# Attention on one core: value products in seven groups a stage instead of ten, with the slots of the exponentials reassigned

## The chip, the cores and the metric

The kernel runs on 1 core of one Trainium2 chip. The metric is the device time of one launch in microseconds (us), the median of several runs. Five engines work side by side and meet at semaphores: TensorE (PE in the rows; PEld is its weight load), VectorE (DVE), ScalarE (ACT), GpSimd (POOL) and SyncE (SP), whose queue issues all transfers.

## The reference, cut to what matters

One block of a transformer: modulated layer norm, latent attention over 1024 positions with 32 heads, a gated residual, a second modulated norm and a feed-forward block. The change touches the attention alone:

```python
scores = jnp.einsum('bqhd,bkhd->bhqk', q_full, k_full) * softmax_scale
scores = jnp.where(causal[None, None], scores, jnp.finfo(scores.dtype).min)
attn = jax.nn.softmax(scores, axis=-1)
out = jnp.einsum('bhqk,bkhd->bqhd', attn, v).reshape(B, S, H * VD)
return out @ wo.T
```

The values of a head are taken in the latent space of 32 numbers a key, so that a key tile's values are 128 keys by 32.

## The kernel before, in words

**Stages, steps, units.** The attention runs in 8 stages (w = 0 to 7), one for each group of 4 heads. A stage has 12 steps (`STEPS`), each one tile of 128 keys against one block of 512 queries. Steps 0 to 3 belong to the first query block, steps 4 to 11 to the second. Causality makes some narrow: their widths in queries are 512, 384, 256, 128 for steps 0 to 3, 512 for steps 4 to 8, and 384, 256, 128 for steps 9, 10, 11. A step is cut into units of 128 queries (times 4 heads, 512 columns), 36 a stage; unit n of a stage is `UNITS[n]`. Step 4 has units 10 to 13, step 5 has 14 to 17, step 6 has 18 to 21, step 7 has 22 to 25, step 8 has 26 to 29, step 9 has 30 to 32, step 10 has 33 and 34, step 11 has 35.

**One step's work.** TensorE makes the scores of a unit with three matmuls (lines 799, 802, 806). ScalarE turns one or two units at a time into exponentials (line 1117). TensorE multiplies them with the values (`values`, line 817): four heads in four bands of 32 rows of PSUM bank 4, each f32 matmul recorded as two instructions, so 8 for a step. VectorE adds the step's exponentials to a running sum (`add`, line 1461). The exponentials of steps 0 and 4 are written straight into the tile of the running sum (`SUM`), so the first addition, that of step 1 or step 5, changes a tile that `values` of step 0 or 4 must have read: it waits for them (`if kt == 1: dve.wait_ge(S_.pv, ...)`). All other steps share two slots (`PR[:, 0]` and `PR[:, 1]`), in turn; the exponential of a step waits until the step before it in its slot has been both multiplied (`S_.pv`) and added (`S_.ad`).

**The order.** Each engine follows one list. In unit n, TensorE does the scores of the unit, then the value products that fall due (`VALUES[n]`, three units after the end of their step, and a step of width 256 held back to go with the next), then side work from a table (`TABLES[w][n]`); VectorE does the additions due (`SUMS[n]`, two units after the end of the step), then the same side work. Before the change `VALUES` stands in ten places of a stage: at unit 2 steps 10 and 11 of the stage before, at 6 step 0, at 9 step 1, at 12 steps 2 and 3, at 16 step 4, at 20 step 5, at 24 step 6, at 28 step 7, at 32 step 8, at 35 step 9.

**Side work.** In stages 0 to 6 it finds the row maxima of the next stage: 38 parts (line 736), each reduced from PSUM by VectorE (line 1369); eight of them are diagonal, and go over ScalarE (line 1062), a mask on GpSimd (line 1703) and VectorE ("least", line 1374). "even", "odd", "lat" and "split" make and rotate the queries of the stage after next, with products on GpSimd ("rotate", lines 1674 and 1675; `split_low`, line 1710). "den" sums the exponentials over the keys (line 749), VectorE copies and inverts the sums (lines 1393, 1398, 1400; "inv"), GpSimd multiplies the result with them ("norm", line 1716). Results of side work on TensorE take three PSUM banks in turn; a piece waits until the piece three places before has been read. "join" and "rows" close the maxima and send them on. A planner (`window_table`) lays the pieces out by a wished place and an estimated cost for VectorE, and moves each "den" to the next unit that has value products.

**Queries rotate in one buffer.** "even" on VectorE waits for `split_low` of the half before (`S_.tl`), since both use `RT`.

Of the kernel before, what the change touches and what calls it, by code (L numbers as in the profile page):

```python
# [14 lines left out]
P = 128  # L15
# [4 lines left out]
G, HG = 8, 4  # L20
# [12 lines left out]
STEPS = [(qb, kt) for qb in range(NQB) for kt in range((qb + 1) * QB // P)]  # L33
NSTEP = len(STEPS)
ADDS = [s for s in range(NSTEP) if STEPS[s][1] > 0]
NADD = len(ADDS)
# [67 lines left out]
def width(s):  # L104
    qb, kt = STEPS[s]
    return min(QB, (qb + 1) * QB - kt * P)


def units_of(s):
    return width(s) // P  # L110
# [13 lines left out]
UNITS = [(s, i) for s in range(NSTEP) for i in range(units_of(s))]  # L124
NUNIT = len(UNITS)
VALUE_LAG, ADD_LAG = 3, 2

HELD = [s for s in range(NSTEP - 1) if units_of(s) == 2]  # L130


def due(n, lag, held=()):

    after = [s + 1 if s in held else s for s in range(NSTEP)]
    return [((n - lag) // NUNIT * -1, s) for s in range(NSTEP)
            if UNITS.index((after[s], units_of(after[s]) - 1)) == (n - lag) % NUNIT]


VALUES = [due(n, VALUE_LAG, HELD) for n in range(NUNIT)]  # L140
SUMS = [due(n, ADD_LAG) for n in range(NUNIT)]
LATE_VALUES = [s for n in range(NUNIT) for ago, s in VALUES[n] if ago]
LATE_SUMS = [s for n in range(NUNIT) for ago, s in SUMS[n] if ago]


def blocks_of(qb):
    return (qb + 1) * QB // P
# [57 lines left out]
class Memory:  # L205
# [167 lines left out]

    def slot(self, s):
        qb, kt = STEPS[s]
        return self.SUM[qb] if kt == 0 else self.PR[:, ADDS.index(s) % 2]

    def out_of(self, g, qb):
        return self.attn[:, g, qb * QB:(qb + 1) * QB]
# [28 lines left out]
def group_places(g, places):  # L408

    return [(place, (name[0], g) + name[1:], 0.0 if name[0] in ("even", "odd") and g in HANDED else busy)  # L410
            for place, name, busy in places]


def window_table(w):

    places = []
    if w == G - 1:
        places += group_places(w, [(0.06 + 0.1 * m, ("fold", m), 1.3) for m in range(G)])
        places += group_places(w, [(0.3 + 0.3 * n, ("gate", n), 2.5) for n in range(2)])
        places += group_places(w, [(0.84 + 0.06 * st, ("high", st), 0.0) for st in range(2)])  # L420
        places += group_places(w, [(0.40 + 0.10 * d, ("mod", 2, d), 0.6) for d in range(KD)])
    else:
        places += group_places(w + 1, maxima_places(0.03, 0.76))
        if w < G - 2:
            places += group_places(w + 2, QUERY_PLACES)
    if w > 0:
        places += [(0.15, ("den", w - 1, 1), 0.7), (0.16, ("inv", w - 1, 1), 0.8), (0.24, ("norm", w - 1, 1), 0.0)]
    places += [(0.42, ("den", w, 0), 0.7), (0.43, ("inv", w, 0), 0.8), (0.50, ("norm", w, 0), 0.0)]
    places.sort(key=lambda x: x[0])
    table = []  # L430
    free = 0.0
    for n in range(NUNIT):
        place = (n + 1) / NUNIT
        for ago, s in SUMS[n]:
            if s in ADDS:
                free = max(free, place) + (HG * width(s) / 960 + 0.07) / WINDOW_US
        names = []
        while places and (n == NUNIT - 1 or max(places[0][0], free - SLACK) <= place):
            _, name, busy = places.pop(0)
            names.append(name)  # L440
            free = max(free, place) + busy / WINDOW_US
        table.append(names)

    for n in range(NUNIT):
        for name in [x for x in table[n] if x[0] == "den"]:
            inverse = ("inv",) + name[1:]
            for names in table:
                if inverse in names:
                    names.remove(inverse)
            table[n].remove(name)  # L450
            m = min(m for m in range(n, NUNIT) if VALUES[m])
            table[m] = [name] + table[m] + [inverse]
    return table


TABLES = [window_table(w) for w in range(G)]
FIRST_FOLDS = [("w", 0)]
FIRST_QUERIES = [[(kind, 0, hf) for kind in ("even", "odd", "lat", "split")] for hf in range(2)]
# [187 lines left out]
def pe_program(nc, M, PS, S_):  # L646
# [163 lines left out]
    def values(w, s):  # L810
        qb, kt = STEPS[s]
        wd = width(s)
        pe.wait_ge(S_.p, NEXP * w + LAST_EXP[s] + 1)
        if kt == 0 and 2 * w + qb > 0:
            pe.wait_ge(S_.o, 2 * w + qb)
        for h in range(HG):
            ins = pe.matmul(PS[h * L:(h + 1) * L, 4, QB - wd:QB], M.V[:, kt, :], M.slot(s)[:, h, 0:wd],  # L817
                            start=(kt == 0), stop=(kt == blocks_of(qb) - 1))
        ins.then_inc(S_.pv, 1)
# [31 lines left out]
    for w in range(G):  # L851
        for n, (s, i) in enumerate(UNITS):
            scores(w, s, i)
            for ago, before in VALUES[n]:
                if ago <= w:
                    values(w - ago, before)
            for name in TABLES[w][n]:
                side(name)

# [26 lines left out]
    for b in range(3):  # L886
        pe.wait_ge(S_.free[b], (len(TURN) + 1 - b) // 3)
    for n, s in enumerate(LATE_VALUES):
        product_term(0, n)
        values(G - 1, s)  # L890
    product_term(1, 0)
    for n in range(len(LATE_VALUES), 3):
        product_term(0, n)
# [66 lines left out]
def act_program(nc, t, M, PS, S_):  # L960
    act = nc.scalar
# [139 lines left out]
    def exponentials(w, e):  # L1101
        s, i, n = EXPS[e]
        qb, kt = STEPS[s]
        turn = NEXP * w + e
        act.wait_ge(S_.sc, turn + 1)
        if i == 0 and kt == 0:
            if w > 0:
                act.wait_ge(S_.side, (DEN0, DEN1)[qb][w - 1] + 1)
        elif i == 0:
            j = ADDS.index(s)  # L1110
            before = NSTEP * w + ADDS[j - 2] - (NSTEP if j < 2 else 0)
            if before > 0:
                act.wait_ge(S_.pv, before + 1)
                act.wait_ge(S_.ad, NADD * w + j - 1)
        banks = PS[:, 2 * (turn % 2):2 * (turn % 2) + n, :].rearrange("p u (h q) -> p u h q", q=P)
        tiles = M.slot(s)[:, :, i * P:(i + n) * P].rearrange("p h (u q) -> p u h q", q=P)
        act.activation(tiles, banks, ACT.Exp).then_inc(S_.p, 1)  # L1117
# [28 lines left out]
    for w in range(G):  # L1146
        for n, (s, i) in enumerate(UNITS):
            e = FIRST_EXP[s] + i // 2
            if i + 1 == EXPS[e][1] + EXPS[e][2]:
                exponentials(w, e)  # L1150
            for ago, before in VALUES[n]:
                if ago <= w and before in (3, NSTEP - 1):
                    empty(w - ago, STEPS[before][0])
            for name in TABLES[w][n]:
                side(name)
# [88 lines left out]
def dve_program(nc, M, PS, S_):  # L1244
# [259 lines left out]
    for w in range(G):  # L1504
        for n in range(NUNIT):
            for ago, s in SUMS[n]:
                if ago <= w and s in ADDS:
# [345 lines left out]
```

## Time and profile before

| | us |
|---|---|
| median of 3 runs (765.14 to 765.54) | 765.2 |
| the profiled execution, its own time | 766.67 |
| its span, first to last instruction | 764.5 |
| TensorE busy in the span | 731.0 (96%) |
| VectorE busy | 542.0 (71%) |
| ScalarE busy | 326.7 (43%) |
| GpSimd busy | 215.4 (28%) |

The busy shares are averages over the whole launch. The granted clock of TensorE is 0.997 of full speed over the span. The eight stages lie between about 90 and 534 us; what follows them is the output projection and the feed-forward block, which the change doesn't touch. In a timeline row the first number is the start, the second the length from first start to last end of the merged instructions, the number behind x their count, and a bracket tells for how long the engine had been idle and which instruction released it. Records of one engine overlap a little, so the time that an instruction takes up is best read from one start to the next.

### The profile page before, as it was taken

The page shows a single profiled execution, that of the slowest core. Times are in us where ns is not written, and L with a number is a line of the kernel's source. Part 1 is how long each engine was busy: PE and PEld are TensorE (multiplying, and loading weights), DVE is VectorE, ACT ScalarE, POOL GpSimd, SP SyncE. Part 2 cuts the span into 40 slices and gives each one's busy share as a digit, 9 for nine tenths or more (in the row PEclk, how much of TensorE's full clock was granted, in tenths as well). Part 3 has the DMA queues.
Part 4 walks back from the last instruction along what each step waited for, and adds up shares of the span by engine and source line. Part 5 has one row for each costly group of instructions (what it writes and reads, how often), then busy time and mean ns, then how long its engine had stood idle before and what let it go on. Part 6 is the DMA issues. An engine that isn't in the chain of part 4 may idle for free.

```text
span 764.5 us, 10504 instructions
## 1 busy us (share of the span) xinstructions
PE 731.0 (96%) x3867; PEld 509.8 (67%) x3867; DVE 542.0 (71%) x803; ACT 326.7 (43%) x499; POOL 215.4 (28%) x196
## 2 busy tenths in 40 slices
PE   3989999999999999999999999999999999999998
PEld 2856676666666666666666666555788888887886
DVE  6867678888888888888888889688695333223432
ACT  4744455545545545545545544444254322222210
POOL 1137635235235235225226121010264000000211
PEclk9999999999999999999999999999999999999999
DMA  8934553303303403303403390360200421200011
GB/s 312 250 72 94 120 118 84 89 11 84 88 12 83 93 7 84 90 11 84 97 3 83 84 358 1 111 220 1 82 23 7 123 71 54 76 10 1 29 41 42
DMA packets 39057, 63.15 MB, mean 83 GB/s; under 512 B 4384, under 2 KB 19232, under 8 KB 37152
## 3 DMA queue, kind: packets, MB, share of 16 engines
q1 hardware_dynamic: 39008, 62.49, 30.3%
q8 instruction: 32, 0.52, 0.3%
q14 instruction: 17, 0.14, 0.1%
HBM read 32.72 MB, written 2.10 MB: 46 GB/s over the span
## 4 chain that ended last, share of the span: by engine, by line
PE 69%; DVE 25%; issue 3%; ACT 2%; DMA 1%; POOL 0%; SPq 0%; DVEq 0%; ACTq 0%; POOLq 0%
PE PS L907 16%; PE PS L924 8%; PE PS L736 8%; DVE PR L1461 7%; PE PS L799 6%; PE PS L817 6%; PE PS L806 5%; PE PS L802 5%; PE PS L871 5%; DVE NMa L1369 4%; DVE wide L1461 3%; PE PS L727 3%; DVE NMd L1374 2%; PE PS L749 2%; PE PS L780 1%
## 5 line engine op out<-in xcount | busy, mean ns | idle before, releaser
L1117 ACT ACTIVATE PR<-PS 128x1024 f32<-128x1024 f32 (+1 forms) x144 | 133.2, 930 | 147.7 <-PE PS L806 116.3
L736 PE MATMUL PS<-KH,Q 96*128 96x128 f32 (+3 forms) x576 | 130.5, 327 | 10.9 <-DVE NMa L1369 5.3
L1369 DVE TENSOR_REDUCE NMa<-PS 128x1 f32<-128x512 f32 (+3 forms) x184 | 116.5, 656 | 29.3 <-PE PS L736 27.4
L736 PEld LDWEIGHTS PS<-KH,Q 96*128 96x128 f32 x576 | 88.8, 190 | 67.3 <-issue 30.7
L799 PE MATMUL PS<-Q,KH 96*128 96x512 f32 x288 | 119.2, 414 | 0.0
L1461 DVE TENSOR_TENSOR PR<-PR 128x2048 f32<-128x2048 f32 (+3 forms) x56 | 112.0, 2000 | 3.9 <-ACT PR L1117 1.5
L806 PE MATMUL PS<-Q,KH 97*128 97x512 f32 (+1 forms) x288 | 114.5, 398 | 0.0
L802 PE MATMUL PS<-Q,KL 96*128 96x512 f32 (+1 forms) x288 | 114.2, 396 | 0.0
L1703 POOL TENSOR_SCALAR_AFFINE_SELECT diag<-diag 128x512 f32<-128x512 f32 x64 | 47.6, 743 | 198.0 <-ACT diag L1062 197.9
L799 PEld LDWEIGHTS PS<-Q,KH 96*128 96x128 f32 x288 | 54.8, 190 | 27.7 <-issue 14.3
L817 PE MATMUL PS<-PR,V 128*32 128x512 f32 (+3 forms) x704 | 70.2, 486 | 0.0
L1585 DVE SCALAR_TENSOR_TENSOR wide<-PS,ffn_s,TQ 128x1024 f32<-128x1024 f32 x10 | 12.8, 1283 | 72.2 <-PE PS L907 72.2
L806 PEld LDWEIGHTS PS<-Q,KH 97*128 97x128 f32 (+1 forms) x288 | 54.6, 190 | 13.2 <-DMA Q<-NM 0.4
L802 PEld LDWEIGHTS PS<-Q,KL 96*128 96x128 f32 (+1 forms) x288 | 54.7, 190 | 8.3
L1062 ACT ACTIVATE diag<-PS 128x512 f32<-128x512 f32 x64 | 38.0, 594 | 46.3 <-PE PS L736 46.3
L907 PE MATMUL PS<-Q 128*128 128x512 f32 x240 | 55.5, 389 | 0.0
L1716 POOL TENSOR_TENSOR wide<-wide,RD 128x512 f32<-128x512 f32 x16 | 34.6, 2164 | 67.4 <-DVE RD L1400 67.4
L1777 POOL TENSOR_TENSOR OT<-TQ,Y 128x512 f32<-128x512 f32 x7 | 9.1, 1294 | 156.7 <-DVE Y L1606 156.7
L907 PEld LDWEIGHTS PS<-Q 128*128 128x128 f32 x240 | 45.0, 188 | 9.3
L907 PE MATMUL PS<-Q,KH 128*128 128x512 f32 (+1 forms) x192 | 49.1, 391 | 0.0
L1374 DVE TENSOR_REDUCE NMd<-diag 128x4 f32<-128x512 f32 x64 | 43.1, 674 | 0.0
L924 PE MATMUL PS<-DH,Q 128*128 128x512 f32 (+1 forms) x176 | 42.6, 390 | 0.0
(185 smaller groups left out, 1088.3 us busy)
## 6 DMA issues: line engine op xcount, KB each, us to landing
Q<-TQ SPq DMA_DIRECT2D x64, 384.0 KB, 6.2
RT<-in_wo SPq DMA_DIRECT2D x4, 1024.0 KB, 4.9
TQ<-in_wo SPq DMA_DIRECT2D x4, 1024.0 KB, 4.8
WI<-in_gate_w SPq DMA_DIRECT2D x10, 256.0 KB, 3.4
WI<-in_up_w SPq DMA_DIRECT2D x10, 256.0 KB, 3.8
DI<-in_down_w SPq DMA_DIRECT2D x10, 256.0 KB, 2.8
PR<-in_wmod_c SPq DMA_DIRECT2D x2, 1024.0 KB, 6.3
x_in<-in_x SPq DMA_DIRECT2D x8, 256.0 KB, 9.7
```

Source lines behind the costliest of these rows:

```text
L736: ins = pe.matmul(bank[:, i * w:(i + 1) * w], M.Q[0:KR, g % 2, 0, qt // 4, h0 + i, qs], M.KH[0:KR, lo:lo + w], start=(i == 0), stop=(i == ...
L799: pe.matmul(dst, M.KH[0:KR, ks], M.Q[0:KR, w % 2, 0, qb, :, qs], start=True, stop=False)
L802: pe.matmul(dst, M.KL[0:rows, ks], M.Q[0:rows, w % 2, 0, qb, :, qs], start=False, stop=False)
L806: ins = pe.matmul(dst, M.KH[0:rows, ks], M.Q[0:rows, w % 2, 1, qb, :, qs], start=False, stop=True)
L817: ins = pe.matmul(PS[h * L:(h + 1) * L, 4, QB - wd:QB], M.V[:, kt, :], M.slot(s)[:, h, 0:wd], start=(kt == 0), stop=(kt == blocks_of(qb) - 1))
L907: ins = pe.matmul(PS[0:m, 4 * b + 2 * w + hf, :], a[b][:, w, k, 0:m], h[:, k, hf * 512:(hf + 1) * 512], start=(n == 0 and k == 0), stop=(n ...
L924: ins = pe.matmul(PS[:, 4 + b, :], a[b][0:k, ch, :], w[0:k, ch, :], start=(n == 0 and ch == 0), stop=(n == 2 and rest == 1))
L1117: act.activation(tiles, banks, ACT.Exp).then_inc(S_.p, 1)
L1369: dve.tensor_reduce(dst, PS[:, bank_of(turn), 0:n * w].rearrange("p (h k) -> p h k", k=w), axis=AX.X, op=ALU.max, negate=True).then_inc(S_ ...
L1374: dve.tensor_reduce(M.NMd[:, qt // 4, :, qt % 4], M.diag[:, qt % 2], axis=AX.X, op=ALU.max, negate=True).then_inc(S_.dm, 1)
L1461: dve.tensor_tensor(sums, sums, M.slot(s)[:, :, 0:wd], ALU.add).then_inc(S_.ad, 1)
L1703: pool.affine_select(out=tile, in_=tile, compare_op=ALU.is_ge, fill=MASKED, base=0, pattern=[[0, HG], [-1, P]], channel_multiplier=1).then ...
```

## The change

Value products stand in seven places of a stage: at unit 2 steps 9, 10 and 11 of the stage before, at 6 step 0, at 12 steps 1, 2 and 3, at 20 steps 4 and 5, at 24 step 6, at 28 step 7, at 32 step 8. In the last stage step 9 stays at unit 35 (`LAST_HELD`).

The two slots are used in another order: one by steps 1, 5, 7, 9, the other by steps 2 and 3 together (side by side, 256 and 128 queries), 6, 8, and 10 and 11 together. So the exponentials of steps 3 and 11 wait for nobody, that of 5 waits for step 1 in place of 2, and those of the others for the same step as before.

The addition of step 5 comes four units after the end of its step 4, at unit 21 in place of 19 (`add_lag`), since the values of step 4 are now taken at unit 20 in place of 16.

The planner's answer follows. In stages 0 to 5 "den" of the first block and its inversion go from unit 16 to unit 20; "least 4", part 24 and "odd" of the second half go from units 20 and 21 to unit 19; parts 25 and 26 from units 21 and 22 to unit 20; "norm" from unit 21 to unit 26, behind `split_low` on GpSimd. Stages 6 and 7 have the same move of "den" and small shifts around it.

```diff
-HELD = [s for s in range(NSTEP - 1) if units_of(s) == 2]
...
+WITH = {1: 3, 2: 3, 4: 5, 9: 11, 10: 11}
+LAST_HELD = 9
+
+SLOTS = ((1, 5, 7, 9), ((2, 3), 6, 8, (10, 11)))
+
+
+def slot_of(s):
+    return 0 if s in SLOTS[0] else 1
+
+
+def used_before(s):
+
+    uses = [use if isinstance(use, tuple) else (use,) for use in SLOTS[slot_of(s)]]
+    n = [s in use for use in uses].index(True)
+    return (uses[n - 1][-1], 1 if n == 0 else 0) if s == uses[n][0] else None
+
+
+def add_lag(s):
+
+    return VALUE_LAG + 1 if STEPS[s][1] == 1 and WITH.get(s - 1) == s else ADD_LAG
...
+VALUES = [due(n, lambda s: VALUE_LAG, WITH) for n in range(NUNIT)]
+SUMS = [due(n, add_lag) for n in range(NUNIT)]
+LATE_VALUES = [s for n in range(NUNIT) for ago, s in VALUES[n] if ago and s != LAST_HELD]
...
-        return self.SUM[qb] if kt == 0 else self.PR[:, ADDS.index(s) % 2]
+        if kt == 0:
+            return self.SUM[qb]
+        lo = 0 if units_of(s) > 1 else 2 * P
+        return self.PR[:, slot_of(s), :, lo:lo + width(s)]
...
-    places += [(0.42, ("den", w, 0), 0.7), (0.43, ("inv", w, 0), 0.8), (0.50, ("norm", w, 0), 0.0)]
+    places += [(0.42, ("den", w, 0), 0.7), (0.43, ("inv", w, 0), 0.8), (0.64, ("norm", w, 0), 0.0)]
...
+            if (w, n) == (G - 1, NUNIT - 1):
+                values(w, LAST_HELD)
...
-        elif i == 0:
-            j = ADDS.index(s)
-            before = NSTEP * w + ADDS[j - 2] - (NSTEP if j < 2 else 0)
-            if before > 0:
-                act.wait_ge(S_.pv, before + 1)
-                act.wait_ge(S_.ad, NADD * w + j - 1)
+        elif i == 0 and used_before(s):
+            before, ago = used_before(s)
+            if w >= ago:
+                act.wait_ge(S_.pv, NSTEP * (w - ago) + before + 1)
+                act.wait_ge(S_.ad, NADD * (w - ago) + ADDS.index(before) + 1)
```

## Rows read from the trace of the kernel before

**Rows 1.** The page: busy time by engine; the chain that ended last, by engine.
```profile
PE 731.0 (96%) x3867; PEld 509.8 (67%) x3867; DVE 542.0 (71%) x803; ACT 326.7 (43%) x499; POOL 215.4 (28%) x196
...
PE 69%; DVE 25%; issue 3%; ACT 2%; DMA 1%; POOL 0%; SPq 0%; DVEq 0%; ACTq 0%; POOLq 0%
```

**Rows 2.** Windows: stage 3, and VectorE's stretch in it; length, then busy PE, PEld, DVE, ACT, POOL.
```profile
259.13:316.27 57.14, 55.58 (x324) 36.29 (x320) 49.92 (x67) 28.77 (x38) 21.64 (x17) 1.00 0.26 60
288.40:312.80 24.40, 23.42 (x121) 15.34 (x121) 23.32 (x32) 12.12 (x15) 13.42 (x9) 1.00 0.29 65
```

**Rows 3.** Timeline of TensorE: value groups at units 12 and 20 of stage 3.
```profile
279.16 0.86 PE L817 MATMUL PS<-PR,V 128*32 128x256 f32 x16
279.95 0.73 PE L736 MATMUL PS<-KH,Q 96*128 96x512 f32 x2
...
292.79 0.39 PE L806 MATMUL PS<-Q,KH 97*128 97x512 f32 x1
293.11 1.06 PE L817 MATMUL PS<-PR,V 128*32 128x512 f32 x8
294.10 0.50 PE L799 MATMUL PS<-Q,KH 96*128 96x512 f32 x1
294.44 0.39 PE L802 MATMUL PS<-Q,KL 96*128 96x512 f32 x1
```

**Rows 4.** Timeline of TensorE: the wait in unit 13, and unit 16 of stage 3.
```profile
281.95 0.66 PE L736 MATMUL PS<-KH,Q 96*128 96x128 f32 x4 [0.57 <-DVE RT L1343]
...
285.88 0.40 PE L802 MATMUL PS<-Q,KL 96*128 96x512 f32 x1
286.11 0.39 PE L806 MATMUL PS<-Q,KH 97*128 97x512 f32 x1
286.43 1.07 PE L817 MATMUL PS<-PR,V 128*32 128x512 f32 x8
287.32 1.04 PE L749 MATMUL PS<-wide,ones 128*32 128x512 f32 x8
288.29 0.94 PE L736 MATMUL PS<-KH,Q 96*128 96x128 f32 x5
```

**Rows 5.** Timeline of VectorE: the first stretch without idle time of stage 3.
```profile
270.49 0.72 DVE L1393 STREAM_TRANSPOSE RD<-PS 128x512 f32<-128x512 f32 x1 [1.49 <-PE PS L749]
...
280.62 0.68 DVE L1342 TENSOR_TENSOR RT<-PS,sin 128x512 f32<-128x512 f32 x1
281.22 0.67 DVE L1343 TENSOR_TENSOR RT<-PS,cos 128x512 f32<-128x512 f32 x1
```

**Rows 6.** Timeline of VectorE: units 16 to 35 of stage 3.
```profile
288.43 0.72 DVE L1393 STREAM_TRANSPOSE RD<-PS 128x512 f32<-128x512 f32 x1 [1.08 <-PE PS L749]
...
293.40 2.28 DVE L1461 TENSOR_TENSOR PR<-PR 128x2048 f32<-128x2048 f32 x1
...
299.92 2.46 DVE L1461 TENSOR_TENSOR PR<-PR 128x2048 f32<-128x2048 f32 x1
...
305.88 3.41 DVE L1461 TENSOR_TENSOR PR<-PR 128x2048 f32<-128x2048 f32 x1
...
310.74 0.67 DVE L1374 TENSOR_REDUCE NMd<-diag 128x4 f32<-128x512 f32 x1
...
312.79 5.47 DVE L1461 TENSOR_TENSOR PR<-PR 128x2048 f32<-128x2048 f32 x3
```

**Rows 7.** Timeline of ScalarE: the exponential of step 10 in stage 3.
```profile
315.19 1.03 ACT L1117 ACTIVATE PR<-PS 128x1024 f32<-128x1024 f32 x1 [1.42 <-DVE PR L1461]
```

**Rows 8.** Timeline of GpSimd in stage 3.
```profile
287.51 2.42 POOL L1710 TENSOR_TENSOR TQ<-RT,TQ 128x1024 fp32r<-128x1024 f32 x1 [2.35 <-ACT TQ L1071]
...
298.94 1.29 POOL L1675 TENSOR_TENSOR RT<-RT 128x512 f32<-128x512 f32 x1
300.18 3.35 POOL L1716 TENSOR_TENSOR wide<-wide,RD 128x512 f32<-128x512 f32 x1
...
304.72 2.42 POOL L1710 TENSOR_TENSOR TQ<-RT,TQ 128x1024 fp32r<-128x1024 f32 x1 [0.31 <-ACT TQ L1071]
```

More of the change, by code:

```diff
@@ L126, with due @@
 VALUE_LAG, ADD_LAG = 3, 2
-HELD = [s for s in range(NSTEP - 1) if units_of(s) == 2]
[L133 to L142, printed above, removed]
+WITH = {1: 3, 2: 3, 4: 5, 9: 11, 10: 11}
[9 more added lines that the diff above has]
+    return VALUE_LAG + 1 if STEPS[s][1] == 1 and WITH.get(s - 1) == s else ADD_LAG
+def due(n, lag, held={}):
+    after = [held.get(s, s) for s in range(NSTEP)]
+    return [((n - lag(s)) // NUNIT * -1, s) for s in range(NSTEP)
+            if UNITS.index((after[s], units_of(after[s]) - 1)) == (n - lag(s)) % NUNIT]
+VALUES = [due(n, lambda s: VALUE_LAG, WITH) for n in range(NUNIT)]
+SUMS = [due(n, add_lag) for n in range(NUNIT)]
+LATE_VALUES = [s for n in range(NUNIT) for ago, s in VALUES[n] if ago and s != LAST_HELD]
 LATE_SUMS = [s for n in range(NUNIT) for ago, s in SUMS[n] if ago]
```

## The prediction, made before the changed kernel ran

> **What bounds the kernel now.** I read the page first [rows 1]: TensorE is busy 96% of the span, yet a quarter of the chain that ended last lies on VectorE. So TensorE is nearly always occupied, but some of its pace is set by VectorE. Then the windows [rows 2]: a stage takes 57.14 us, with VectorE busy for 49.92 of it. In the 24.40 us from unit 16 to the end of unit 32 it is busy for 23.32: there it has 1.08 us to spare, and TensorE has about as much (23.42 busy). Last I followed stage 3 row by row. Three links carry the stage round:
>
> - The first scores of a stage need the bank that the exponential of step 10 empties. That exponential starts when VectorE has added step 8, whose slot it takes, at 315.19, and ends at 316.22 [rows 7]. The next stage begins at 316.27 [rows 2]. TensorE's own work, with the values of step 9 as its last piece, ends at the same moment.
> - "den" of the stage before, at unit 6, starts a stretch of VectorE without a gap from 270.49 to 281.8 [rows 5], after which TensorE has waited 0.57 us for a bank in unit 13 [rows 4].
> - "den" of unit 16 is copied at 288.43, and 24.36 us later, at 312.79, VectorE starts the addition of step 8 [rows 6], which leads to the first link.
>
> **What a group costs.** Ordinary matmuls follow each other every 0.23 us [rows 4]. A 512-wide step followed at once by "den" takes 0.89 us (286.43 to 287.32), so 128 queries cost 0.22. Between ordinary matmuls, the step of unit 20 takes 1.65 from 292.79 to 294.44 [rows 3]; less two ordinary ones (0.46) and the step itself (0.88) this leaves 0.31 us for going into the narrow form and out again. The pair of unit 12 takes 0.79 for 384 queries [rows 3], no more than its columns and one passage need. A group of three is not in the trace; its joints cost between nothing and 0.31 each, and by the pair I take nothing. The bands of 32 are a tiling mode, and the Trainium skill (TensorEngine Tiling (Array Packing), Key Properties) says that changing the mode drains TensorE; the trace agrees with its 0.31.
>
> Fewer groups remove passages at units 9, 16 and 35 in stages 0 to 6. In stage 7 a "fold" in the same narrow form stands behind the values at 9 and 16, and step 9 stays at 35, so nothing is removed there. That is 21 passages, 6.5 us of TensorE, if nobody else sets the pace.
>
> **Where that goes: the start of a stage.** The values of step 9 (384 queries, 0.66 us) leave unit 35 and enter unit 2. At the boundary their leaving gives nothing, since the exponential of step 10 ends at 316.22 anyway. In unit 2 they lengthen a stretch that TensorE paces: VectorE had been idle 1.49 us when "den" reached it [rows 5]. So "den" comes 0.65 us later, VectorE's stretch ends 0.65 later, and unit 13 resumes at 282.60 in place of 281.95. The passage saved at unit 9 only lengthens the wait in unit 13.
>
> **The middle.** Unit 16 ends its scores at 286.34 + 0.65 = 286.99 (one pitch behind 286.11 [rows 4]) and has no values or "den". What stood between 288.29 and 293.11, the parts of units 16 to 18, "even" and the scores of units 17 to 20, takes 4.82 - 0.10 of passage. Part 24 and "odd" join in unit 19: four matmuls of 128 columns and three of 512, about 1.15 us (an estimate from 0.1 and 0.23 each and the joints). One wait is near: "even" may not start before the first half's `split_low` has ended. That was 289.93 [rows 8], becomes 290.58, and comes about 0.45 later than "even" would like; before it was no limit. So the values of step 4 start at about 286.99 + 4.72 + 1.15 + 0.10 + 0.45 = 293.4. From there to VectorE's copy of "den" it was 2.00 us (286.43 to 288.43); with step 5 in between it is 2.88. The copy starts at 296.3.
>
> VectorE meanwhile does "even" from 290.65, part 23, "least 4" and "odd": six instructions at 0.60 from start to start [rows 5], until 294.3. Here it used to add step 5 (293.40 [rows 6]). That addition must now wait for the values of step 4, which have moved from unit 16 to unit 20, and the queue puts it at unit 21, behind "den". VectorE stands still for 2.0 us, in the half of the stage where it had 1.08 to spare. This is the step on which the forecast turns.
>
> From the copy to the addition of step 8: 24.36 before. Parts 21, 22, 23, "even", "least 4" and "odd" now lie ahead of it (eight instructions at 0.60, and 0.05 between two: -4.9). The 1.08 idle goes, as the pieces are ready by then. The additions of steps 6 and 7 took 2.46 and 3.41 against 2.28 for that of step 5 [rows 6], because two-operand work of VectorE and GpSimd on SBUF excludes each other: that of step 6 began when rotation ended at 300.23, that of step 7 when `split_low` ended at 307.14 [rows 8]. Rotation is now earlier (-0.18), and `split_low` ends just as VectorE comes to step 7 (-1.13). "norm" follows `split_low` on GpSimd now, then the mask of the last diagonal, so "least 7" waits some 0.3. Sum: 24.36 - 4.9 - 1.08 - 1.31 + 0.3 = 17.4; the addition of step 8 starts at 313.7 in place of 312.8, and the stage is 0.85 us longer. TensorE keeps up; its saved passages turn into waiting. The sending of the maxima at the end of the stage is shifted with VectorE and stays covered.
>
> **The sum.** Stages 1 to 5: 5 x 0.85 = 4.25. Stage 0 has nothing at unit 2: 0.85 - 0.65 = 0.2. Stage 6 has no queries to rotate and a freer VectorE: between all of TensorE's gain (-0.93 for three passages, -0.66 for step 9 handed on) and +0.85; midway, -0.4. Stage 7 takes over step 9 (+0.65), and the late addition of step 5 holds up the exponential of step 7 for between 0 and 1.1 (what exclusion by "norm" costs, 3.41 less 2.28); I take 0.4. Together +5.1 us: span 764.5 to 769.6, the profiled time 766.67 to about 771.8. The profiled execution lies 1.5 above the median, so the median goes from 765.2 to 770.3.
>
> **The rivals.**
> - *TensorE's gain arrives* (faster). If VectorE can absorb its gap, all 21 passages count: 765.2 - 6.5 = 758.7. For it: TensorE is 96% busy, and exponentials 3 and 11 lose their waits. Against it: 23.32 of 24.40, and the boundary at 316.22. It decides if "den" of unit 20 is copied before about 294.5, so that the gap stays under 0.3 us. Then stages 1 to 5 end 0.9 us or more earlier than I have them.
> - *It cancels.* Half of the gap is made up: 1.0 less a stage for five stages gives 765.3.
> - *"norm" gets in first* (slower still). VectorE reaches step 7 at the very time when `split_low` ends. At 300.23 the waiting addition got ahead of a "norm" that stood behind rotation (its record starts at 300.18 and runs 3.35 [rows 8]). If the addition comes a moment too late, "norm" goes first: +1.29 for it, less the 0.3 of "least 7", in stages 0 to 5: 770.3 + 6 = 776.3. The Trainium skill (SBUF — State Buffer, SBUF: two separate sides) states that whichever starts first has the shared pair of ports for the whole instruction; the order at 300.23 agrees, since the addition had been issued first, and by it the outcome hangs on less than 0.3 us.
>
> **How the numbers follow.** Within 0.2% (763.7 to 766.7) is about what measurement can't tell from no change. My case has 0.40 and a range of its own of 767 to 773; "norm" first 0.16; TensorE's gain wholly or in part 0.28; cancelled 0.16. Below 760 I see 0.10 and above 776 another 0.09, so the range is 760 to 776. Faster 0.28, same 0.16, slower 0.56.
>
> **What the changed profile would show.** Right: in stages 1 to 5 a period near 58.0 in place of 57.14; VectorE idle about 2 us before L1393 of unit 20; the addition of step 5 about 5 us later in the stage; TensorE waiting some 0.8 us before the first scores of a stage; TensorE's busy time 5 to 6 us lower. "norm" first: the addition of step 7 at 3.4 us or more while L1716 runs. Wrong: no gap at unit 20, or a period of 56.5 or less. What would make it wrong above all: side work that VectorE finds ready in unit 19 and 20 later than I have it on TensorE's clock, or earlier.

## The result, and the profile after

The changed kernel takes 786.5 us (median of 4 runs, 784.18 to 786.74) where the kernel before took 765.2. The ratio is 1.0271, with a 95% interval of 1.0258 to 1.0284: slower by 21 us, and outside the range of 760 to 776. The profiled execution took 786.35 us with a span of 784.1, so the span grew by 19.6 us. The page after has these rows against those of [rows 1]: busy time by engine, and the last chain by engine.

```profile
PE 732.1 (93%) x3867; PEld 514.2 (66%) x3867; DVE 539.1 (69%) x803; ACT 323.9 (41%) x499; POOL 214.3 (27%) x196
...
PE 64%; DVE 25%; issue 4%; ACT 4%; POOL 2%; DMA 1%; SPq 0%; DVEq 0%; ACTq 0%; POOLq 0%
```

TensorE fell from 96% to 93% of the span: it waits more. Its busy time did not fall by the 5 to 6 us that fewer passages should have given; it rose by 1.1. The windows of stages 3 and 4 show why (length, busy PE, PEld, DVE, ACT, POOL, then the granted clock of TensorE):

```profile
266.70:325.70 59.00, 54.81 (x321) 36.73 (x320) 48.83 (x66) 28.34 (x38) 20.67 (x17) 1.00 0.26 60
325.70:386.00 60.30, 56.40 (x321) 37.25 (x320) 50.30 (x68) 28.34 (x38) 20.68 (x17) 0.97 0.26 59
```

In stage 3 TensorE is busy 54.81 us, 0.77 less than in [rows 2], where three passages at the forecast price would be 0.93. But the stage takes 59.0 where it took 57.14. Stage 4 is another 1.3 us longer and is the only one of the two with a mean clock below 1.00. These are two separate losses.

**The gap at unit 20 came as forecast.** VectorE in stage 3 after, to be held against [rows 6]:

```profile
297.62 0.69 DVE L1356 TENSOR_TENSOR RT<-PS,cos 128x512 f32<-128x512 f32 x1 [1.20 <-POOL TQ L1731]
...
300.61 0.68 DVE L1364 TENSOR_TENSOR RT<-PS,cos 128x512 f32<-128x512 f32 x1
303.42 0.72 DVE L1414 STREAM_TRANSPOSE RD<-PS 128x512 f32<-128x512 f32 x1 [2.12 <-PE PS L769]
...
306.13 2.25 DVE L1482 TENSOR_TENSOR PR<-PR 128x2048 f32<-128x2048 f32 x1
...
308.90 2.28 DVE L1482 TENSOR_TENSOR PR<-PR 128x2048 f32<-128x2048 f32 x1
...
314.68 3.42 DVE L1482 TENSOR_TENSOR PR<-PR 128x2048 f32<-128x2048 f32 x1
...
321.60 5.48 DVE L1482 TENSOR_TENSOR PR<-PR 128x2048 f32<-128x2048 f32 x3
```

Line 1482 is the addition (1461 before) and 1414 the copy of "den" (1393 before). VectorE is idle 2.12 us before the copy. (The 1.20 before "even", line 1356, is its wait for the `split_low` of the half before; the prediction had 0.45.) The additions of steps 5 and 6 take 2.25 and 2.28, unhindered. That of step 7 takes 3.42. GpSimd at that moment:

```profile
312.29 2.42 POOL L1731 TENSOR_TENSOR TQ<-RT,TQ 128x1024 fp32r<-128x1024 f32 x1
314.67 1.28 POOL L1737 TENSOR_TENSOR wide<-wide,RD 128x512 f32<-128x512 f32 x1
316.40 2.19 POOL L1724 TENSOR_SCALAR_AFFINE_SELECT diag<-diag 128x512 f32<-128x512 f32 x1 [0.45 <-ACT diag L1084]
```

The record of "norm" (line 1737) begins where `split_low` (line 1731) ends, at 314.67, and VectorE's addition begins at 314.68. "norm" takes its usual 1.28 us and the addition takes 1.14 more than the one before. All six stages with a `split` (0 to 5) show the same: the record of "norm" begins 0.01 to 0.03 us ahead of the addition's, and the addition takes 3.40 to 3.42. This is the rival *"norm" gets in first*, to which I had given 0.16 and a time of 776.3.

**The granted clock falls.** TensorE in stage 2, and the windows of 3.4 us on both sides of 260.2:

```profile
258.48 0.91 PE L756 MATMUL PS<-KH,Q 96*128 96x384 f32 x2 [1.17 <-DVE NMa L1390]
...
259.93 0.39 PE L819 MATMUL PS<-Q,KH 96*128 96x512 f32 x1
...
260.52 0.63 PE L826 MATMUL PS<-Q,KH 97*128 97x512 f32 x1
261.08 1.94 PE L837 MATMUL PS<-PR,V 128*32 128x512 f32 x8
```
```profile
256.80:260.20 3.40, 2.21 (x10) 1.33 (x9) 3.40 (x6) 0.60 (x2) 1.53 (x1) 1.00 0.00 0
260.20:263.60 3.40, 3.40 (x14) 0.99 (x13) 3.23 (x5) 1.77 (x3) 0.00 (x0) 0.50 0.02 5
```

TensorE waited 1.17 us for a reduction of VectorE, in unit 30. Soon after, the clock goes from full speed (2.4 GHz) to half (1.2 GHz) for 3.4 us: a matmul takes 0.63 instead of 0.39, the eight of step 8 take 1.94 instead of 1.06. It happens in stages 0, 2 and 4 (at 140.8, 260.2 and 379.7), and in stage 6 it lasts twice 3.4 us (from 461.6). The profiled execution of the kernel before had one such fall, in stage 6 at 465.9. Stages 1, 3 and 5 have a like wait (1.18, 1.18 and 1.15) and no fall. How many falls there are also differs between executions of one program: three of the four after have a mean clock of 0.988 or 0.989 and take 786.35 to 786.74 us, the fourth has 0.993 and takes 784.18.

### The profile page after: what moved, and what is told of

It reads as the page before. It is cut to its first block, busy times and chain, and to the rows that moved or that the text cites. A ratio compares the mean times of both kernels' runs of the same rounds, so it can differ in the third digit from the quotient of the medians.

```text
span 784.1 us, 10487 instructions
## 1 busy us (share of the span) xinstructions
PE 732.1 (93%) x3867; PEld 514.2 (66%) x3867; DVE 539.1 (69%) x803; ACT 323.9 (41%) x499; POOL 214.3 (27%) x196
## 4 chain that ended last, share of the span: by engine, by line
PE 64%; DVE 25%; issue 4%; ACT 4%; POOL 2%; DMA 1%; SPq 0%; DVEq 0%; ACTq 0%; POOLq 0%
PE PS L929 15%; DVE PR L1482 8%; PE PS L946 8%; PE PS L837 7%; PE PS L756 6%; PE PS L819 5%; PE PS L893 5%; DVE NMa L1390 4%; PE PS L826 4%; PE PS L822 4%; PE PS L747 3%; DVE wide L1482 2%; POOL TQ L1731 2%; PE PS L769 2%; DVE NMb L1390 2%
## 5 line engine op out<-in xcount | busy, mean ns | idle before, releaser
L756 PE MATMUL PS<-KH,Q 96*128 96x128 f32 (+3 forms) x576 | 128.0, 327 | 22.2 <-DVE NMa L1390 14.5
L1482 DVE TENSOR_TENSOR PR<-PR 128x2048 f32<-128x2048 f32 (+3 forms) x56 | 109.0, 1946 | 4.8 <-ACT PR L1138 2.7
L1724 POOL TENSOR_SCALAR_AFFINE_SELECT diag<-diag 128x512 f32<-128x512 f32 x64 | 54.9, 858 | 205.0 <-ACT diag L1084 205.0
L1737 POOL TENSOR_TENSOR wide<-wide,RD 128x512 f32<-128x512 f32 x16 | 25.7, 1606 | 69.2 <-DVE RD L1421 69.2
```

The costliest lines, as they stand in the source:

```text
L756: ins = pe.matmul(bank[:, i * w:(i + 1) * w], M.Q[0:KR, g % 2, 0, qt // 4, h0 + i, qs], M.KH[0:KR, lo:lo + w], start=(i == 0), stop=(i == ...
L1482: dve.tensor_tensor(sums, sums, M.slot(s)[:, :, 0:wd], ALU.add).then_inc(S_.ad, 1)
L1724: pool.affine_select(out=tile, in_=tile, compare_op=ALU.is_ge, fill=MASKED, base=0, pattern=[[0, HG], [-1, P]], channel_multiplier=1).then ...
```

## The experiments

I measured a stage by the time from one copy of the second block's "den" (unit 6) to the next. The first column is the start of the first of these copies; all in us.

| kernel | first | stage 1 | 2 | 3 | 4 | 5 | 6 | 7 | half clock in stages |
|---|---|---|---|---|---|---|---|---|---|
| before | 156.17 | 57.16 | 57.16 | 57.13 | 57.13 | 56.23 | 52.40 | 45.55 | 6 |
| after | 158.76 | 59.02 | 60.27 | 59.02 | 60.24 | 58.06 | 55.55 | 47.59 | 0, 2, 4, 6 (twice as long) |
| step 4 apart | 156.61 | 57.82 | 57.80 | 57.79 | 57.79 | 56.90 | 53.07 | 45.56 | 6 |
| "norm" late | 157.06 | 57.86 | 57.85 | 57.89 | 57.90 | 56.94 | 53.99 | 47.62 | 6 |
| waits filled | 157.87 | 58.96 | 58.97 | 58.97 | 58.96 | 58.06 | 54.94 | 47.62 | 6 |
| step 9 at home | 156.77 | 59.90 | 58.33 | 58.34 | 59.87 | 57.41 | 53.73 | 47.62 | 1, 4, 6 |
| `split` late | 154.93 | 56.03 | 56.04 | 56.01 | 56.02 | 55.12 | 50.86 | 45.58 | none |

The last column is what one profiled execution shows, not a constant of the kernel. A copy's period is named by the stage in which it begins, so the fall in stage 2, at 260.2, lies in the period of 60.27, and that of stage 0 in the first column.

**1. The joining of steps 4 and 5 undone** (`b_step4_apart`). The changed kernel without `4: 5`; "norm" goes back to its old place.

```diff
-WITH = {1: 3, 2: 3, 4: 5, 9: 11, 10: 11}
+WITH = {1: 3, 2: 3, 9: 11, 10: 11}
...
-    places += [(0.42, ("den", w, 0), 0.7), (0.43, ("inv", w, 0), 0.8), (0.64, ("norm", w, 0), 0.0)]
+    places += [(0.42, ("den", w, 0), 0.7), (0.43, ("inv", w, 0), 0.8), (0.50, ("norm", w, 0), 0.0)]
```

> The changed kernel, but the values of step 4 back at unit 16, the addition of step 5 back at unit 19, den at 16 and norm at 21 as before: eight groups a stage; steps 1 to 3 stay together at unit 12 and steps 9 to 11 at unit 2. Theory (VectorE's 2.1 us of standing still at unit 20, the exclusion by norm and the falls of TensorE's clock that follow TensorE's waits make the loss): VectorE has no gap at unit 20, and a stage costs only the 0.65 us of step 9 at unit 2: about 57.8 a stage in place of 57.14, no fall of the clock in stages 0 to 5, 767 to 770 us. Rival (the handing of step 9 over the stage's boundary is the main loss): 780 us or more.

Measured: 770.48 us, ratio 1.0063 (1.0048 to 1.0078). The stage takes 57.80 us, the gap before the copy is back at 1.09, and the falls of stages 0, 2 and 4 are gone. So three quarters of the loss come with the joining of steps 4 and 5 and with the place that "norm" then has, and what is left, 0.65 us a stage, is step 9 in unit 2, the term that I had for it. The collision of the kernel before is still in this kernel: its addition of step 7 takes 3.41.

**2. Step 9 at home** (`c_step9_home`). The opposite: steps 4 and 5 joined, step 9 at unit 35 in every stage, `LAST_HELD` gone.

```diff
-WITH = {1: 3, 2: 3, 4: 5, 9: 11, 10: 11}
+WITH = {1: 3, 2: 3, 4: 5, 10: 11}
```

> The changed kernel, but the values of step 9 back at unit 35 of their own stage: eight groups a stage; steps 4 and 5 stay together at unit 20. Theory: stages 1 to 5 get back 0.65 us each and stage 7 as much, VectorE's gap of 2.1 us at unit 20 stays: 781 to 784 us. Rival (step 9 over the boundary is the main loss): 765 to 770 us.

Measured: 780.11, ratio 1.0194 (1.0179 to 1.0209). A stage without a fall takes 58.33, 0.69 less than after. The time lies 0.9 under the range that I had expected; this profiled execution has two falls in stages 0 to 5, that of the changed kernel three. The falls are now in stages 1 and 4: they move with the timing, and aren't tied to certain stages.

**3. "norm" behind the last mask** (`d_norm_late`). All of the change, but "norm" of the first block moves from unit 26 to unit 28, behind part 32, in stages 0 to 5, and from unit 24 to 25 in stage 6.

```diff
-    places += [(0.42, ("den", w, 0), 0.7), (0.43, ("inv", w, 0), 0.8), (0.64, ("norm", w, 0), 0.0)]
+    places += [(0.42, ("den", w, 0), 0.7), (0.43, ("inv", w, 0), 0.8), (0.66, ("norm", w, 0), 0.0)]
```

> The changed kernel with norm of the first block one place later in stages 0 to 5, behind the mask of the last diagonal on GpSimd (unit 28 in place of 26), so that it can't stand between split_low and the addition of step 7. Theory: the addition of step 7 takes 2.3 us in place of 3.4, each of these stages is 1.0 us shorter (58.0 in place of 59.0): 780.5 us; if the shorter wait of TensorE behind it also does away with the falls of its clock, 776.5 us. Rival (norm's place doesn't matter, the loss lies in VectorE's gap alone): 786 us.

Measured: 775.40, ratio 1.0128 (1.0113 to 1.0143): 11.1 us faster than the change as it stood, with one number moved. That is 1.1 more than I had expected even without falls; stage 6, which I had left out, gained 0.95. VectorE and then GpSimd in stage 3 of this kernel:

```profile
307.02 1.88 DVE L1390 TENSOR_REDUCE NMa<-PS 128x1 f32<-128x512 f32 x3
308.81 0.68 DVE L1395 TENSOR_REDUCE NMd<-diag 128x4 f32<-128x512 f32 x1
309.40 2.28 DVE L1482 TENSOR_TENSOR PR<-PR 128x2048 f32<-128x2048 f32 x1
...
314.87 0.18 DVE L1402 TENSOR_TENSOR NMa<-NMa,NMb 128x16 f32<-128x16 f32 x1
```
```profile
307.02 2.41 POOL L1731 TENSOR_TENSOR TQ<-RT,TQ 128x1024 fp32r<-128x1024 f32 x1
311.12 1.06 POOL L1724 TENSOR_SCALAR_AFFINE_SELECT diag<-diag 128x512 f32<-128x512 f32 x1 [1.69 <-ACT diag L1084]
312.15 1.27 POOL L1737 TENSOR_TENSOR wide<-wide,RD 128x512 f32<-128x512 f32 x1
```

`split_low` ends at 309.43, and the addition of step 7 takes 2.28. From the copy of "den" to the addition of step 8 VectorE needs 17.05 us (298.14 to 315.19); I had summed 17.4. In the changed kernel it is 18.18 (303.42 to 321.60), longer by the 1.13 of exclusion. With that gone, TensorE's wait of 1.17 at unit 30 is gone too (no wait of 0.5 us or more is left there), and stages 0 to 5 of the profiled execution have no fall. Waits of 0.7 to 0.94 elsewhere in these stages stay. Two of the four executions have a clock of 0.994 and 0.995, lower than the 0.997 of the profiled one.

**4. TensorE's waits filled** (`e_fill`). The changed kernel, with matmuls into a free PSUM bank just before the waits: three at unit 26 and four at unit 30, in stages 0 to 6. Their results are overwritten by the scores that belong there; the computation is unchanged.

```diff
+            if n in (26, 30) and w < G - 1:
+                turn = NEXP * w + FIRST_EXP[s]
+                for _ in range(3 if n == 26 else 4):
+                    pe.matmul(PS[:, 2 * (turn % 2) + 1, :], M.KH[0:KR, 0:P], M.Q[0:KR, w % 2, 0, 1, :, 0:P], start=True, stop=True)
```

> The changed kernel with 3 matmuls more at unit 26 and 4 more at unit 30 in stages 0 to 6, into the bank that the next unit's scores overwrite; they lie in TensorE's waits for VectorE of 0.8 and 1.2 us there. Theory (the three falls of the clock to half speed in stages 0, 2 and 4 come of these waits and cost 1.25 us each): no fall in stages 0 to 5, the stages take 59.0 each without exception: 782 to 784 us. Rival (the falls have nothing to do with the waits): they stay, and the extra work costs nothing or a little: 786 to 789 us.

Measured: 782.15, ratio 1.0220 (1.0203 to 1.0237), 4.35 us faster than the change with more work on TensorE. TensorE in stage 3, with the four added matmuls in the first row:

```profile
315.14 1.09 PE L882 MATMUL PS<-Q,KH 96*128 96x512 f32 x4
316.45 0.91 PE L756 MATMUL PS<-KH,Q 96*128 96x384 f32 x2 [0.21 <-DVE NMa L1395]
```

All stages 1 to 4 now take 58.96 to 58.97. Against 60.27 and 60.24 that is 1.3 us a fall. VectorE's chain was not made shorter, so this price is the clock's alone. (In experiment 2 a fall costs 1.5 to 1.6: 59.90 and 59.87 against 58.33.) The fall of stage 6, behind a wait of 1.40 that was not filled, stays. The four executions have clocks of 0.996 to 0.998, against 0.988 to 0.993 of the change.

**5. `split` of the kernel before moved** (`h_split_late`). The exclusion at step 7 is already there in the kernel before: 3.41 us in [rows 6], where the addition came upon the `split_low` that starts at 304.72 [rows 8]. Here is the kernel before with one number changed, so that `split` of the second half stands behind part 32 in unit 28:

```diff
-                 (0.47, ("even", 1), 1.2), (0.50, ("odd", 1), 1.2), (0.55, ("lat", 1), 1.3), (0.60, ("split", 1), 0.0)]
+                 (0.47, ("even", 1), 1.2), (0.50, ("odd", 1), 1.2), (0.55, ("lat", 1), 1.3), (0.66, ("split", 1), 0.0)]
```

> The kernel before, its values untouched, but split of the second half on ScalarE and GpSimd behind the mask of the last diagonal (unit 28 in place of 26) in stages 0 to 5, so that it does not exclude the addition of step 7. Theory (VectorE sets the pace from unit 17 to 32): that addition takes 2.3 us in place of 3.4, and as TensorE has 0.75 and 0.21 us of waits there to give back, each of six stages is 0.7 to 1.0 us shorter: 759.5 to 761 us. Rival (TensorE sets the pace, exclusion of VectorE is hidden): 765 us.

Measured: 758.28, ratio 0.9906 (0.9892 to 0.9919). This kernel beats both, and lies 1.2 under my range. Its stage 3, VectorE and GpSimd:

```profile
302.40 2.27 DVE L1461 TENSOR_TENSOR PR<-PR 128x2048 f32<-128x2048 f32 x1
```
```profile
304.52 0.64 POOL L1703 TENSOR_SCALAR_AFFINE_SELECT diag<-diag 128x512 f32<-128x512 f32 x1 [3.58 <-ACT diag L1062]
305.47 2.42 POOL L1710 TENSOR_TENSOR TQ<-RT,TQ 128x1024 fp32r<-128x1024 f32 x1 [0.31 <-ACT TQ L1071]
```

The addition takes 1.14 less, and the stage 1.1 less (56.03). So these 1.1 us of VectorE's are 1.1 us of the stage, with no change in the work of TensorE.

**6. One passage more, where TensorE sets the pace** (`j_step10_apart`). The kernel before; the values of step 10 get a group of their own.

```diff
-HELD = [s for s in range(NSTEP - 1) if units_of(s) == 2]
+HELD = [2]
```

> The kernel before, but the values of step 10 at unit 1 of the next stage, not with those of step 11 at unit 2: eleven groups a stage, one passage more in a stretch that TensorE paces. Both theories: each stage from 1 on starts its den 0.3 us later and is 0.3 us longer (57.4 in place of 57.14), 7 x 0.31 = 2.2 us: 767.4. If a passage is hidden or cheaper here: under 766.

Measured: 767.87, ratio 1.0035 (1.0022 to 1.0049). Stages 1 to 4 take 57.46 to 57.64: a passage costs 0.3 to 0.5 us here, 0.34 in stage 2 (57.16 to 57.50). I had 0.31.

**7. One passage more, ahead of the wait in unit 13** (`k_step2_apart`). The kernel before; the values of step 2 get a group of their own.

```diff
-HELD = [s for s in range(NSTEP - 1) if units_of(s) == 2]
+HELD = [10]
```

> The kernel before, but the values of step 2 at unit 11, not with those of step 3 at unit 12: eleven groups a stage, one passage more in a stretch where TensorE waits 0.57 us for VectorE behind it (unit 13). Theory: the passage shortens that wait and costs nothing: stages of 57.1 us, 765.0 to 766.0. Rival (a passage is 0.31 us wherever it stands): 8 x 0.31 = 2.5 us more, 767.7.

Measured: 766.04, ratio 1.0006 (0.9997 to 1.0015), stage 57.14. Here the same passage costs the stage nothing.

**8. Only step 1 joined to steps 2 and 3** (`f_step1_joined`). The changed slots with other groups; "norm" at 0.50 and no `LAST_HELD`.

```diff
-WITH = {1: 3, 2: 3, 4: 5, 9: 11, 10: 11}
+WITH = {1: 3, 2: 3, 10: 11}
```

> The changed kernel with only one of its three joinings: the values of step 1 taken with those of steps 2 and 3 at unit 12 (nine groups a stage). Step 4 is back at 16, step 9 at 35, norm at 21; the new slots stay. Theory (the passage saved at unit 9 only lengthens TensorE's wait for VectorE in unit 13, and the slots do nothing): stages 0 to 5 stay at 57.1 us, the whole within 0.2% of before, 764 to 766.5. Rival (a passage saved is 0.31 us saved): 7 x 0.31 less, 763.0.

Measured: 766.42, ratio 1.0014 (1.0004 to 1.0023), stage 57.16. The passage saved at unit 9 is lost in the wait of unit 13, as forecast. The median is even 1.2 above the 765.25 of the kernel before beside it, and the granted clock goes with it: it is under 0.999 in 8 of the 12 executions, against 3 of 23 of the kernel before and 1 of 11 in experiment 9, which differs from this one only in the joining. The four executions at 1.0 take 764.8 to 765.4. The profiled one is among these, so where the falls lie isn't shown.

**9. Only the slots changed** (`a_slots`). As 8, with the groups of the kernel before.

```diff
-WITH = {1: 3, 2: 3, 4: 5, 9: 11, 10: 11}
+WITH = {2: 3, 10: 11}
```

> The kernel before with the new slots alone (steps 2 and 3 side by side, 10 and 11 side by side; exponentials 3 and 11 wait for nobody); value products in ten groups at their old units. Theory (no engine that sets the pace waits for these exponentials): 57.1 us a stage, 764.5 to 766. Rival (the new slots cost or give something of their own): more than 1 us away from before.

Measured: 765.07, ratio 0.9994 (0.9985 to 1.0003), stage 57.14. The order of the slots alone is worth nothing, either way.

**10. Experiments 8 and 5 together** (`l_step1_split_late`).

```diff
-                 (0.47, ("even", 1), 1.2), (0.50, ("odd", 1), 1.2), (0.55, ("lat", 1), 1.3), (0.60, ("split", 1), 0.0)]
+                 (0.47, ("even", 1), 1.2), (0.50, ("odd", 1), 1.2), (0.55, ("lat", 1), 1.3), (0.66, ("split", 1), 0.0)]
```

> The faster kernel with the late split (758.3 us, stages of 56.03) and the joining of step 1 with steps 2 and 3, the only one of the three joinings that cost nothing alone; new slots. Theory (VectorE still sets the pace in both halves of the stage): no gain, stages of 56.0, 757.5 to 759. Rival (with VectorE freed by 1.1 us a stage, TensorE's passage counts): 56.0 - 0.31 a stage, 756.

Measured: 759.5, ratio 0.9919 (0.9903 to 0.9935), stage 56.01: no better than `split` late alone, at 56.03. That is 0.5 above my range. The profiled execution has one fall, in stage 6, which `split` late alone has not; the clock is under 0.999 in 3 of 5 executions here and in none of 4 there. Even with VectorE 1.1 us shorter the passage at unit 9 brings nothing.

**11. The change with "norm" and `split` both late** (`m_change_both_late`), at 0.66 both.

```diff
-    places += [(0.42, ("den", w, 0), 0.7), (0.43, ("inv", w, 0), 0.8), (0.64, ("norm", w, 0), 0.0)]
+    places += [(0.42, ("den", w, 0), 0.7), (0.43, ("inv", w, 0), 0.8), (0.66, ("norm", w, 0), 0.0)]
...
-                 (0.47, ("even", 1), 1.2), (0.50, ("odd", 1), 1.2), (0.55, ("lat", 1), 1.3), (0.60, ("split", 1), 0.0)]
+                 (0.47, ("even", 1), 1.2), (0.50, ("odd", 1), 1.2), (0.55, ("lat", 1), 1.3), (0.66, ("split", 1), 0.0)]
```

> The changed kernel with split of the second half and norm both behind the mask of the last diagonal: nothing of GpSimd stands before the addition of step 7. Theory: split already ended just as VectorE came to step 7 in the run with norm alone moved (775.4 us, stages of 57.87), so there is little left: 774 to 776. It then stands 1.8 us a stage above the kernel before with the late split (56.03), which is what the change costs when exclusion is out of both: 0.65 at unit 2 and some 1.2 for VectorE's standing still. Rival (the late split helps the changed kernel as it helps the other): 768.

Measured: 779.27, ratio 1.0180 (1.0161 to 1.0199). I expected 774 to 776; a miss, and of the kind that the study is about. The stage takes 58.66 where "norm" late alone takes 57.87. VectorE and GpSimd in stage 3:

```profile
315.25 1.01 DVE L1390 TENSOR_REDUCE NMb<-PS 128x1 f32<-128x384 f32 x2
316.39 0.96 DVE L1402 TENSOR_TENSOR NMa<-NMa,NMb 128x16 f32<-128x16 f32 x1
```
```profile
316.04 1.28 POOL L1737 TENSOR_TENSOR wide<-wide,RD 128x512 f32<-128x512 f32 x1
```

With `split_low` ahead of it, "norm" now runs from 316.04 to 317.32, over "join" (line 1402). That is an operation of 16 columns, 0.18 us long in experiment 3, and 0.96 here. It has two operands in SBUF, and it stands directly before the addition of step 8. The whole difference of 0.79 is that.

**12. "gate" of stage 7 later** (`p_gate_late`). Experiment 3, with the second "gate" of the last stage moved from unit 21 to 25, to free VectorE between the additions of steps 5 and 6.

```diff
-        places += group_places(w, [(0.3 + 0.3 * n, ("gate", n), 2.5) for n in range(2)])
+        places += group_places(w, [(0.3 + 0.42 * n, ("gate", n), 2.5) for n in range(2)])
```

> The changed kernel with norm behind the last diagonal (775.4 us), and in stage 7 the floor of the second gate (four instructions, 2.7 us on VectorE) four units later, so that the addition of step 6 follows that of step 5 at once. Theory for stage 7 (its 2.07 us come from exponentials that wait for late additions on VectorE, not from the joined groups themselves): 1 to 2 us less, 773.5 to 774.5. Rival (they come from the groups): 775.4.

Measured: 777.03, ratio 1.0149 (1.0129 to 1.0168): slower by 1.6 than experiment 3, not faster. TensorE's only wait before the end of stage 7, in experiment 3 and then here:

```profile
533.93 0.50 PE L819 MATMUL PS<-Q,KH 96*128 96x512 f32 x1 [1.37 <-ACT PR L1138]
```
```profile
535.07 0.50 PE L819 MATMUL PS<-Q,KH 96*128 96x512 f32 x1 [2.04 <-ACT PR L1138]
```

The wait grew from 1.37 to 2.04, and the clock fell behind it at 536.9. The planner had moved other pieces along with the one that I meant: "gate" now stood before the addition of step 7 instead, and another operation ("mod", 1.77 us beside GpSimd) between 5 and 6. So the addition of step 6 starts 1.6 us earlier in the period, but that of step 7 ends where it did. TensorE resumes 34.43 us after the period's first copy here (500.64 to 535.07) and 34.44 in experiment 3 (499.49 to 533.93). The period is 1.51 longer all the same (49.13 against 47.62), so its loss lies behind the wait, and a fall of the clock, which experiment 3 doesn't have in this stage, costs about as much. The profiled execution also has the clock at half for twice 3.4 us from 72.4 on, ahead of the attention; two of the four executions have its clock of 0.991, the other two 0.995. So this run doesn't test what I meant it to test: whether the second "gate" is the cause stays open.

## Why the prediction was wrong, step by step

**The account.** The chain of experiments 1, 3 and 4 splits the 19.6 us of span into four steps, each the difference of two profiled executions:

| from, to | span | worth | what it is |
|---|---|---|---|
| before, step 4 apart | 764.5, 768.9 | 4.4 | step 9 in unit 2 |
| step 4 apart, "norm" late | 768.9, 772.6 | 3.7 | steps 4 and 5 joined, and no collision (3.41 in the first, 2.28 in the second) |
| "norm" late, waits filled | 772.6, 779.9 | 7.3 | "norm" ahead of the addition of step 7 |
| waits filled, after | 779.9, 784.1 | 4.2 | the clock at half speed |

The third has the few added matmuls in it, and what "norm" does in stage 6 (0.95). By the medians (765.7, 770.5, 775.4, 782.2, 786.5) the four are worth 4.8, 4.9, 6.8 and 4.3. The first two make 8.1 us, where the forecast had 5.1. Stages 0 to 5 are not where the 3.0 are missing: the first scores of stage 6 come at 430.55 before and at 434.42 with "norm" late, 3.9 later, and I had 4.25 + 0.2. Those of stage 7 come at 483.23 and 488.71. So stage 6 is 1.6 longer, where I had -0.4, and stage 7 is 2.7 longer, where I had 0.65 + 0.4. So the 14.5 us above the forecast are three things: 7.3 for "norm", 4.2 for the clock, 3.0 for the last two stages (3.6 there, less 0.6 in stages 0 to 5). The rival alone, at 776.3, would not have reached 786.5 either.

**The step that failed.** It is first of all this one: "`split_low` ends just as VectorE comes to step 7 (-1.13)". I had seen that the two ends lie together and took the gain all the same, with "norm" queued directly behind `split_low`. In the profile after they are 0.01 us apart (314.67 and 314.68), and "norm" goes first. I priced the outcome, at 6 us for six stages, and there it cost 6.3; but my sum took the other one, and 0.16 was too low a chance for a tie within 0.3 us. Nothing in the rows of before spoke for the addition more than for "norm": at 300.23 it had been waiting for 0.3 us already. The Trainium skill (SBUF — State Buffer, SBUF: two separate sides) states that whichever of the two starts first holds the shared pair for its whole instruction. The trace agrees: "norm" starts first by 0.01 to 0.03 us, and the addition takes 3.42 against 2.28 us.

Two more terms failed: the clock, which I had put at nothing without a reason (4.2), and the terms of stages 6 and 7, -0.4 and +1.05, which measured 1.6 and 2.7. Both are taken up below.

The place of "norm" was also a choice. The section on the change calls it the planner's answer, but the diff moves its wished place from 0.50 to 0.64. No run has the change with "norm" at 0.50, so what it would cost there isn't known. (The same section puts the addition of step 5 four units after the end of step 4; it is four units after the end of step 5, unit 17.)

**The middle of the stage, otherwise.** The gap was 2.12 us (forecast 2.0), the additions of steps 5 and 6 took 2.25 and 2.28 as assumed, and without "norm" VectorE needed 17.05 from the copy to the addition of step 8 (forecast 17.4). The stage without collision and fall takes 57.87, against 58.0 forecast. The reading that VectorE can't absorb a gap here held: experiment 5 moves the stage by all of the 1.1 us that it saves VectorE, and experiment 11 by the 0.8 that it adds.

**The start of the stage.** Step 9 in unit 2 costs 0.65 a stage, as forecast (57.80 less 57.14). Passages saved at unit 9 bring nothing, as forecast (experiments 8 and 10). The price of a passage, 0.31, measured 0.3 to 0.5 where TensorE sets the pace (experiment 6) and nothing elsewhere (experiment 7). That a group of three has free joints holds too. TensorE at unit 12 of stage 3 after, 768 queries in one group:

```profile
286.75 1.50 PE L837 MATMUL PS<-PR,V 128*32 128x384 f32 x24
288.19 0.74 PE L756 MATMUL PS<-KH,Q 96*128 96x512 f32 x2
```

They take 1.44 us, 0.24 for 128 queries with the passage in it; by the 0.22 of the prediction and one passage it would have been 1.63. So TensorE did save most of what was counted, 0.77 of 0.93 us in stage 3, and turned it into waiting.

**The clock.** It was in no step, and it is 4.2 of the 19.6 us. The row that could have warned was in the trace of before: in stage 6, behind a wait of 0.62 us, the clock fell at 465.9.

```profile
464.74 1.09 PE L736 MATMUL PS<-KH,Q 96*128 96x512 f32 x2 [0.62 <-DVE NMb L1369]
465.67 0.45 PE L799 MATMUL PS<-Q,KH 96*128 96x512 f32 x1
465.92 0.63 PE L802 MATMUL PS<-Q,KL 96*128 96x512 f32 x1
```

I had the mean of 0.997 over the span and drew nothing from it. It was not the usual state either: of the 45 executions of the kernel before that were measured beside the experiments, 40 have a clock of 0.999 or more. The profiled one took 1.5 us more than the median, about the price of one fall, so between the medians, 21.3 us apart, the clock's part is larger than 4.2; I estimate some 6 us (three falls of 1.3 in stages 0 to 4; the 1.5 of the profiled execution before, for the fall of stage 6; 0.6 for its double length). A change that gives TensorE waits of over 1 us can pay for them twice.

**Stages 6 and 7.** I had -0.4 in stage 6 and, for stage 7, +0.65 for step 9 and +0.4 for the late addition. By the periods of the table, stage 6 is 3.15 longer: 0.65 for step 9 (part of 53.07), 0.9 for steps 4 and 5 (53.99), 0.95 for "norm" (54.94) and 0.6 for the longer time at half clock (55.55). The freer VectorE of that stage saved nothing, so the "midway" of my sum was wrong. Stage 7 is 2.04 longer, and the loss is in every version that joins steps 4 and 5 (47.6 or more) and in none that doesn't (45.5 to 45.9). TensorE in stage 7 after, where before there was no wait:

```profile
545.34 0.50 PE L819 MATMUL PS<-Q,KH 96*128 96x512 f32 x1 [1.38 <-ACT PR L1138]
```
```profile
544.26 1.51 ACT L1138 ACTIVATE PR<-PS 128x1024 f32<-128x1024 f32 x2 [1.69 <-DVE PR L1482]
```

The wait is 1.38, above the 1.1 that I had as the end of the term's bound, and it is not for the exponential of step 7, which I had named. It is for that of step 9 (the ScalarE row), which waits for the addition of step 7. VectorE is idle 3.68 us before the copy of "den" in this stage, against 1.45 before, and the addition of step 7 ends 33.1 us into the period, against 30.2. The other 0.64 is busy time of TensorE (46.19 against 45.55 in that window). About half of it is a narrow form more: I had said that nothing is removed in stage 7, but from unit 6 on four "fold" now stand alone where one did, and two groups of values less make up for only two of the three. What the rest is, and whether another order of the side work would remove the wait, stays open.

**What stays open besides.** Which wait brings the clock down. A wait of 0.62 stood before a fall in one execution of the kernel before, waits of 1.18 stood before none in stages 1 and 3 after. That filling the waits of stages 0 to 5 removes their falls is shown; what decides from stage to stage, and from execution to execution, is not.

**The faster version.** Of the twelve, `split` late on the kernel before is the best, at 758.3 us against 765.2. The best with the change's groups of 4 and 5 is 775.4.

## What to carry to other kernels

Where two engines exclude each other, look at what stands in both queues at the end of each stretch, and let no operation off the path stand ready just when one on the path comes: moving a single entry behind the next mask was worth 7 us to the kernel before and 11 to the changed one (some of it the clock's), while moving both entries of the changed one cost 4 of these again, because a tiny operation on the path (0.18 us) was then held up by 0.8. Fewer and larger groups save only where their engine sets the pace, and they make results later for everybody else; count the second before the first. A wait on TensorE costs its length and, if the granted clock falls behind it, over a us more.

## What the runs showed of the hardware that I had not expected

- Where GpSimd had a next instruction queued behind the one that ended, and VectorE's came within 0.03 us, GpSimd's went ahead in six stages of six: 1.28 us for GpSimd, 3.42 in place of 2.28 for VectorE, in the changed kernel.
- A mask on GpSimd, with one input in SBUF, takes 0.64 us alone and 2.19 beside the two-operand addition that started 1.7 us before it.
- An operation of 16 columns on VectorE grew from 0.18 to 0.96 us beside "norm".
- The granted clock of TensorE fell to half for 3.4 us behind waits of 0.6 to 2.0 us, at 1.2 to 1.6 us each time, in some stages and executions and not in others that look the same.
